# Softmax rows divided on ScalarE before the transpose, the residual added by TensorE, and the energies put ahead of the transposes

## The reference

```python
# L2
energy = jnp.einsum('bci,bcj->bij', q, k)
attention = jax.nn.softmax(energy, axis=-1)
out = jnp.einsum('bcj,bij->bci', v, attention)
out = gamma[0] * out + xf
# L3
scores = jnp.einsum('nia,nib->nab', theta, phi) / jnp.sqrt(jnp.float32(c))
attn = jax.nn.softmax(scores, axis=-1)
f = jnp.einsum('nab,nib->nia', attn, g)
```

## Time and profile before

| | |
|---|---|
| median of 3 runs | 5754.26 us |
| the profiled execution | 5758.38 us, of which 5756.6 us lie between its first and last instruction |
| VectorE busy | 5060.5 us (88%) |
| TensorE busy | 4756.3 us (83%) |
| GpSimd busy | 4706.1 us (82%) |
| ScalarE busy | 3713.5 us (65%) |
| TensorE's mean granted clock | 0.929 |

### The profile page before, as it was taken

One profiled execution on the slowest core, in us unless ns is written; L12 is line 12 of the kernel. 1 busy time (PEld: TensorE's weight loads), 2 busy tenths in 40 slices (PEclk: granted clock), 3 DMA queues, 4 the chain that ended last, 5 costly groups with the idle time before them and its releaser, 6 DMA issues.

```text
span 5756.6 us, 61917 instructions
## 1 busy us (share of the span) xinstructions
PE 4756.3 (83%) x17331; PEld 2758.9 (48%) x17331; DVE 5060.5 (88%) x5978; ACT 3713.5 (65%) x6077; POOL 4706.1 (82%) x3342
## 2 busy tenths in 40 slices
PE   6568888888888888888888888888888888888771
PEld 6134554555445445545554454455455544544451
DVE  4689999999999999999999999999999999999933
ACT  3456666667666666666676667666766766666633
POOL 0698988888888888888888988888888889888910
PEclk9679999999999999999999999999999999999995
DMA  4456555555565555656655655655566566555527
GB/s 130 182 219 223 221 201 218 220 220 211 217 220 211 209 221 216 218 208 220 220 204 219 223 215 211 218 216 204 219 220 220 208 219 225 212 207 219 214 82 295
DMA packets 199099, 1216.87 MB, mean 211 GB/s; under 512 B 27880, under 2 KB 28656, under 8 KB 67696
## 3 DMA queue, kind: packets, MB, share of 16 engines
q1 hardware_dynamic: 194416, 1196.26, 56.6%
q10 hardware_dynamic: 4352, 16.78, 0.7%
HBM read 1158.43 MB, written 54.53 MB: 211 GB/s over the span
## 4 chain that ended last, share of the span: by engine, by line
PE 34%; DVE 29%; issue 14%; ACT 12%; POOL 8%; DMA 1%; DVEq 1%; SPq 0%; POOLq 0%; ACTq 0%
DVE hs L488 12%; PE psE L814 12%; DVE psD L484 11%; PE psA L814 10%; PE psT L814 6%; POOL pa L300 5%; DVE nm L513 3%; PE psT L987 3%; ACT da L680 3%; ACT p L726 3%; PE psY L814 2%; DVE psU L477 1%; POOL pa L306 1%; ACT L649 1%; ACT L751 1%
## 5 line engine op out<-in xcount | busy, mean ns | idle before, releaser
L300 POOL TENSOR_TENSOR pa<-hs,rows_all 128x1024 f32<-128x1024 f32 x1024 | 2411.3, 2355 | 522.7 <-DVE hs L488 522.2
L680 ACT ACTIVATE da<-delta,neg_a 128x512 f32<-128x512 f32 x2048 | 1375.7, 715 | 224.9 <-DVE hs L488 212.6
L484 DVE TENSOR_TENSOR psD<-rows_all,psU 128x512 f32<-128x512 f32 x2048 | 1415.9, 691 | 84.6 <-POOL hlast L304 6.0
L488 DVE TENSOR_TENSOR_SCAN hs<-da,hlast,psD 128x512 f32<-128x512 f32 x1024 | 1310.8, 1280 | 36.3
L306 POOL TENSOR_TENSOR pa<-pa 128x512 f32<-128x512 f32 x1024 | 1301.2, 1271 | 40.1
L488 DVE TENSOR_TENSOR_SCAN hs<-da,psD 128x512 f32<-128x512 f32 x1024 | 1249.2, 1220 | 35.2
L726 ACT ACTIVATE p<-psE,nm 128x1024 f32<-128x1024 f32 x512 | 569.6, 1113 | 633.8 <-DVE nm L513 633.8
L814 PE MATMUL psA<-pt,va 128*128 128x256 f32 x4096 | 954.2, 381 | 1.0 <-DVE x L531 0.6
L814 PEld LDWEIGHTS psA<-pt,va 128*128 128x128 f32 x4096 | 772.5, 192 | 194.9 <-issue 105.9
L513 DVE TENSOR_REDUCE nm<-psE 128x1 f32<-128x1024 f32 x512 | 618.6, 1208 | 275.5 <-PE psE L814 272.3
L690 ACT ACTIVATE pt<-psT 128x512 f32<-128x512 f32 x1024 | 554.9, 591 | 342.5 <-PE psT L987 332.8
(11 more groups left out here) (186 smaller groups left out, 5087.6 us busy)
## 6 DMA issues: line engine op xcount, KB each, us to landing
rows_all<-bc_scratch SPq DMA_DIRECT2D x1024, 1024.0 KB, 4.7
xin<-x SPq DMA_DIRECT2D x40, 512.0 KB, 7.8
xres<-x SPq DMA_DIRECT2D x64, 256.0 KB, 6.3
x_scratch<-x SPq DMA_DIRECT2D x32, 512.0 KB, 4.2
f_scratch<-fa SPq DMA_DIRECT2D x32, 512.0 KB, 6.8
xres<-x SPq DMA_DIRECT2D x8, 512.0 KB, 3.7
x1g<-x SPq DMA_DIRECT2D x8, 512.0 KB, 3.6
fa<-x SPq DMA_DIRECT2D x8, 512.0 KB, 3.7
```

What stands on the lines that cost most here:

```text
L300: pool.tensor_tensor(pa[:, k % PROD, :, :], hs[:, sl, :, :], rows_all[:, slot, 2:4, :], ALU.mult).then_inc(S["prod"], 1)
L484: dve.tensor_tensor(psD[:, :], rows_all[:, slot, j, :], psU[:, :], ALU.mult).then_inc(S["dbu_ok"], 1)
L488: dve.tensor_tensor_scan(hs[:, sl, j, :], da[:, sl, j, :], psD[:, :], hlast[:, h, n_:n_ + 1] if ch else 0.0, ALU.mult, ALU.add).then_inc(S ...
L680: act.activation(da[:, k % 2, j, :], delta[:, h, cols(ch)], ACT.Exp, scale=neg_a[:, h, 2 * q + j:2 * q + j + 1]).then_inc(S["da_ok"], 1)
```

## The change

- ScalarE multiplies the exponentials `p` of each tile in place by the reciprocals of their row sums (`scale`, 128x1024, 16 times an image), before TensorE transposes them. The transpose waits for it (semaphore `scaled`).
- VectorE takes one reciprocal column for a tile (16 an image, where it took two columns for a group, 8 an image), and takes it inside a step, between the second product and the second scan. For that `scans` is split into `inputs` and `states`.
- TensorE no longer spreads the reciprocals. For m = 0 it adds the residual x1g into psA with one matmul of 256 columns for a group; gamma goes into the values.
- ScalarE copies the finished group from psA to `x2` or `fa` (`weighed`), where it copied `rb`. VectorE keeps only `bn_stats` for m = 1.
- `ORDER`: the energy of a step stands ahead of the transpose, of `steps` and of `centre`.

```diff
-        RECIP_AT = [10, 13, 15, 18]
+        RECIP_AT = [8, 9, 11, 12, 14, 15, 17, 18]
...
                 def normalise(a, o):
-                    for m, gq in groups_at(RECIP_AT, o):
-                        i = NG // 2 * m + gq
-                        pair = slice(GT * (i % 2), GT * (i % 2) + GT)
-                        wait(dve, "p_ok", a, GT * (i + 1))
-                        wait(dve, "av_mm", a, i - 1)
-                        dve.reciprocal(rinv[:, pair], rsum[:, pair]).then_inc(S["rinv_ok"], 1)
+                    for m, t in tiles_at(RECIP_AT, o):
+                        i = TILES * m + t
+                        sl = slice(i % (2 * GT), i % (2 * GT) + 1)
+                        wait(dve, "p_ok", a, i + 1)
+                        wait(dve, "scaled", a, i - 2 * GT + 1)
+                        dve.reciprocal(rinv[:, sl], rsum[:, sl]).then_inc(S["rinv_ok"], 1)
...
-                        wait(dve, "av_mm", a, i + 1)
-                        wait(dve, "rb_ok", a, i + 1)
-                        if m == 0:
...
-                            dve.scalar_tensor_tensor(out=psA[:, 0:GL], in0=psA[:, 0:GL], scalar=c_gam, in1=rb[:, :],
-                                                     op0=ALU.mult, op1=ALU.mult).then_inc(S["scaled"], 1)
-                            wait(dve, "scaled", a, gq + 1)
-                            dve.tensor_tensor(x2[:, part], psA[:, 0:GL], x1g[:, part], ALU.add).then_inc(S["out_ok"], 1)
-                        else:
...
-                            dve.tensor_tensor(fa[:, part], psA[:, 0:GL], rb[:, :], ALU.mult
-                                              ).then_inc(S["out_ok"], 1)
+                        if m == 1:
...
+                def scale(a, o):
+                    for m, t in tiles_at(RECIP_AT, o):
+                        i = TILES * m + t
+                        rs = i % (2 * GT)
+                        wait(act, "rinv_ok", a, i + 1)
+                        act.activation(p[:, i % 2, :], p[:, i % 2, :], ACT.Copy, scale=rinv[:, rs:rs + 1]
+                                       ).then_inc(S["scaled"], 1)
+
+                def weighed(a, o):
...
-                        act.activation(rb[:, :], psA[:, GL:2 * GL], ACT.Copy).then_inc(S["rb_ok"], 1)
...
+                        act.activation((x2, fa)[m][:, part], psA[:, 0:GL], ACT.Copy).then_inc(S["out_ok"], 1)
...
                             for a, o in now:
+                                scale(a, o)
                                 turned_out(a, o)
...
                 def turn(a, m, t, front):
                     i = TILES * m + t
-                    wait(pe, "p_ok", a, i + 1)
+                    wait(pe, "scaled", a, i + 1)
...
                     if half:
-                        wait(pe, "rinv_ok", a, i + 1)
-                        for u in range(GT):
-                            rs = (GT * i + u) % (2 * GT)
-                            last = mm(psA[:, GL + 128 * u:GL + 128 * u + 128], rinv[:, rs:rs + 1].to_broadcast([128, 128]),
-                                      ident[:, :])
+                        if m == 0:
+                            wait(pe, "x1g_ok", a, NCH)
+                            last = mm(psA[:, 0:GL], ident[:, :], x1g[:, gq * GL:(gq + 1) * GL], start=False)
...
-                    "centre energy add variance",
-                    "energy turn add weigh0",
-                    "weigh1 turn add residual",
+                    "centre add variance",
+                    "add energy weigh0 turn",
+                    "weigh1 residual turn add",
...
-                    "steps energy add weigh0",
-                    "turn weigh1 turn_more skip1 add",
-                    "energy add",
-                    "energy turn weigh0 add",
-                    "turn weigh1 add",
+                    "add energy steps weigh0",
+                    "weigh1 turn skip1 turn_more add energy_next",
+                    "add",
+                    "weigh0 energy turn add",
+                    "weigh1 turn add energy_next",
```

More of the change, by code:

```diff
@@ L232, in build, with tiles_at @@
         TURN_AT = [8, 10, 12, 12, 14, 15, 17, 18]
-        RECIP_AT = [10, 13, 15, 18]
+        RECIP_AT = [8, 9, 11, 12, 14, 15, 17, 18]
         WEIGH_AT = [(11, 12), (14, 15), (17, 18), (19, 19)]
         ATTEND_AT = [13, 16, 18, 20]
+        def tiles_at(table, o):
+            return [(m, t) for m in range(2) for t in range(TILES) if 16 * m + table[t] == o]
         def turned_at(o):
-            return [(m, t) for m in range(2) for t in range(TILES) if 16 * m + TURN_AT[t] == o]
+            return tiles_at(TURN_AT, o)
         def groups_at(table, o):
@@ L468, in normed, with inputs @@
                     dve.tensor_tensor(xn[:, KC - 1 + fc * CH:KC - 1 + fc * CH + CH], xcen[:, :], rstd[:, :], ALU.mult).then_inc(S["xn_ok"], 1)
-                def scans(b, k, j):
+                def inputs(b, k, j):
                     ch, r = divmod(k, NS)
@@ L549, in image @@
                             if scan:
-                                scans(b, k, 0)
+                                inputs(b, k, 0)
+                                states(b, k, 0)
                             if front_of and r == AT_N:
                                 normed(*front_of)
-                            for a, o in now:
-                                normalise(a, o)
                             if att and k == 2:
@@ L561, in image @@
                             if scan:
-                                scans(b, k, 1)
+                                inputs(b, k, 1)
+                            for a, o in now:
+                                normalise(a, o)
+                            if scan:
+                                states(b, k, 1)
                             for a, o in now:
@@ L754, in image @@
                             for a, o in now:
-                                spread(a, o)
+                                weighed(a, o)
                             if att and k == 5:
@@ L999, in values @@
                     for j in range(TB // 2 * half, TB // 2 * (half + 1)):
[L1000 removed]
+                        last = mm(psA[:, 0:GL], va[:, j, :], pt[:, i % 2, j, :], start=(j == 0),
+                                  stop=(j == TB - 1 and m == 1))
                     if half:
[L1002 to L1006 removed]
+                        if m == 0:
+                            wait(pe, "x1g_ok", a, NCH)
+                            last = mm(psA[:, 0:GL], ident[:, :], x1g[:, gq * GL:(gq + 1) * GL], start=False)
                         last.then_inc(S["av_mm"], 1)
@@ L1044, in _ @@
                     "energy add",
-                    "energy turn add skip0",
-                    "gates add",
-                    "energy rows turn add",
-                    "steps energy add weigh0",
-                    "turn weigh1 turn_more skip1 add",
-                    "energy add",
-                    "energy turn weigh0 add",
-                    "turn weigh1 add",
+                    "skip0 energy turn add",
+                    "gates add energy_next",
+                    "rows turn add",
+                    "add energy steps weigh0",
[3 more added lines that the diff above has]
+                    "weigh1 turn add energy_next",
                 ]
@@ L1102, in work @@
                                             energy(a, *TILE_STEP[o], scan)
+                                        if what == "energy_next" and o + 1 in TILE_STEP:
+                                            energy(a, *TILE_STEP[o + 1], scan)
                                         if what in ("turn", "turn_more"):
```

30 lines of the change are left out of this document (16 added, 14 removed).

## The result

The changed kernel takes 5865.78 us (median of 6 runs, 5857.75 to 5871.87) against 5754.37 us of the kernel before beside it: a ratio of 1.0198, with a 95% interval of 1.0184 to 1.0211. It is slower by 111 us, where I had forecast 56. The time lies inside the range.

The account below looks back on a forecast made before the run. Bound by VectorE's summed work and, in steps 7 to 17, a loop between engines. Per image 2.3 + 2.0 + 2 x 0.8 - 2.4 - 1.7 = +1.8 us; 31 images +56, so 5810 us; range 5650 to 5880.

Parts of the forecast that it names:

- the side: Whole kernel: the change makes it slower, chance 0.50, against 0.14 for the same and 0.36 for faster.
- the loop: Steps 7 to 17 of each attention: energy, maximum, exponential, next energy set the end; seven scalings enter it.
- stretch A: End of tile 0's maximum to start of tile 4's: 2.3 us longer for m = 0, 2.0 for m = 1.
- stretch B: End of tile 4's maximum to start of tile 7's, 20.2 us before: 0.8 us longer in each attention.
- the gain of VectorE's queue: Work and waits that VectorE loses, less the new reciprocals: 201 us less if its queue set the end everywhere.
- The wait that I named: VectorE at tile 3's reciprocal, for sums of ScalarE's exponential: 1.7 us; all reciprocal waits some 80 to 150 us.
- stretch C: End of tile 7's maximum to start of the next attention's tile 0: -2.4 us for m = 0, -1.7 for m = 1.
- the clock: Tile 3's energy on TensorE, after a longer idle time: kept at 3.25 us, where another energy took 1.88.
- Rival 1: Clock stays up, energies of tiles 3 and 6 at full rate: -3.0 us an image, 5661 us; chance 0.22.
- `steps`: Step 11, now behind tile 3's energy: four activations end at 25.0 us, tile 3's exponential follows at 26.1, before 22.4.

Follow-up runs that it names:

- experiment 4: Changed kernel with the matmuls of `steps` put ahead of tile 3's energy again in step 11: 5776.96 us, ratio 1.0046.
- experiment 11: Kernel of experiment 5 with ScalarE's four activations of step 11 moved behind the exponential of tile 3: 5715.71 us, ratio 0.9934.
- experiment 9: Kernel of experiment 5 with ScalarE's scaling cut to 2 of the 1024 columns of each tile: 5659.9 us, ratio 0.9838.
- experiment 5: Changed kernel with tile 7's energy put ahead of `add` in step 17: 5802.12 us, ratio 1.0085.
- experiment 8: Changed kernel with four added, unused matmuls of 256 columns ahead of tile 3's energy in step 11: 5784.56 us, ratio 1.0059.
- experiment 7: Kernel before, with only the line of step 11 changed, so `add` and tile 3's energy stand ahead of `steps`: 5651.35 us, ratio 0.9823.
- experiment 10: Kernel before with the changed table ORDER, except step 17, which stays as it was: 5765.61 us, ratio 1.0023.
- experiment 3: Changed kernel with ScalarE's scaling cut to 2 of the 1024 columns of each tile: 5803.15 us, ratio 1.0094.

## Why the prediction was right and wrong

**Right: the side, the loop, and the length of stretches A and B; this in part by luck.** I had said that the gain of VectorE's queue would be given back where a tile's energy, maximum, exponential and scaling hang in a ring. Stretch A grew by 1.9 us (forecast 2.15) and B by 0.8 (0.8). The wait that I named, at the reciprocal of tile 3, is the largest. All waits before reciprocals are 214.3 us, where I had said 80 to 150. Experiments 4 and 11 undo its cause from two sides, TensorE's and ScalarE's, and the wait goes in both; they win 89 and 86 us, of which a part comes by other ways (stretch B in 11, and perhaps the clock in 4). The pass takes 1.148 us by the trace of the changed kernel (1.14 forecast), and its length costs 142 us in the kernel of experiment 9.

Luck has a share in three places. In A of m = 0 I had the energy of tile 3 1.2 us too long (3.25 for 2.07 in the mean), and the stretch is only 0.5 us shorter than forecast, so some 0.7 us of the other sign are not found. In A of m = 1 I had read one attention, 30.96 us, where the mean is 32.2; the changed kernel has 34.2 for the 33.0 of the forecast, so both ends were 1.2 us short and the difference came out. In B the +0.8 stood for energies at the low clock, but those of tiles 6 and 7 take 2.2 and 1.8 us. The maxima of these tiles wait 0.9 and 0.8 us for them in the mean, and tile 7's wait goes when its energy stands ahead of `add` (experiment 5).

**Wrong: the size of stretch C.** The step reads "m = 0: [...] 25.7 us, with TensorE ready at 25.3; -2.4" and "m = 1: [...] ready at 26.7; -1.7". It measured 27.2 in both, -0.8. Nothing of VectorE's saving counts there beyond what TensorE lets through; the maximum of tile 0 waits 1.05 and 1.44 us for its energy. I had TensorE's queue too short by 1.9 us in m = 0 and by 0.5 in m = 1. The trace of the kernel before shows it, in the same stretch of m = 0:

```profile
3109.73 1.96 PE L814 MATMUL psT<-x,tp_t 128*128 128x512 f32 x4 [0.88 <-issue]
...
3118.26 1.96 PE L814 MATMUL psE<-ka,x 128*128 128x512 f32 x4
```

Tile 0's energy ends at 3120.2, 27.8 us after the maximum of tile 7, and VectorE takes it at 28.1. So TensorE was only 0.3 us ahead before the change, and the change takes 0.6 us out of its queue (27.8 to 27.2), where I had it fall to 25.3. I left out the 0.88 us in which it waits, between the convolution and `project`, until ScalarE has emptied psT; in the changed kernel that copy is this row of ScalarE, and TensorE goes on at 3001.12:

```profile
3000.34 0.69 ACT L638 ACTIVATE xc<-psT,cbias 128x512 f32<-128x512 f32 x1 [4.08 <-PE psT L825]
```

The other 1.0 us I put down to small pieces (the edge columns, the residual's matmul, two short waits), without a row for each. That term is (2.4 + 1.7 - 1.6) x 31 = 77 us. Some 16 of it come from the one image that I had read, whose two stretches C, 28.1 and 28.4 us, are 0.5 us longer together than the means. The other differences have the other sign: A was 0.25 us an attention too dear, 16 us, and some 16 us come back outside the images. 77 - 16 - 16 = 45, the miss between the profiled executions (102 us for 56).

**Half right: the clock.** I let the energy of tile 3 run at 3.25 us in every attention. Over 57 attentions it takes 2.4 us, less than before the change, so this was too dark. What I had left out is what comes after it: `steps` and the first group at half rate, which in m = 1 put the four activations and the exponential of tile 3 later still. In sum the low clock in step 11 costs 81 us (experiment 8). Rival 1, with the clock up, was to give 5661 us; with the clock up in step 11 the kernel takes 5785. Its part A comes out in sum (+1.3 and -0.2 us, where it had +0.7 and +0.4), C was too short there as well (77 us), and B is 0.8 us longer than before, where it had nothing (50 us).

**Half right: `steps`.** In the prediction this line of the order only costs. In the changed kernel it does. In the kernel before the line wins 99 us (experiment 7), so it is bad only together with something that the change brings. That this is the scaling in its shadow is likely and not shown: the two orders were not compared with a short scaling, and `add` moved too. My theory for that experiment fell.

**The order and the division.** Alone, the order costs 127 us and the division 364. The order's loss in the kernel before is mainly step 17, 112 us, where tile 7's energy stands behind GpSimd's sum; I had that wait in part B, with nothing won as its price. In the changed kernel the swap wins 64 us, but most of it in stretch A (experiment 5). The line of step 2 costs 20 us, and those of steps 12, 14 and 15 cost 20. Of the 114 us that are left besides step 17, about 74 stay open: they lie in the lines of steps 0 and 8 (the energy ahead of `centre`, `skip0` first) or in the lines together. By the stretches, most of the 114 us are in C: 29.1 us in experiment 10, 27.4 in experiment 7.

## What to carry to other kernels

When work is moved off the busiest engine, look where it lands in the ring of waits, not at how busy the engine there is: ScalarE only went from 65% to 72%, and yet a pass of 1.15 us between an exponential and its transpose, with the waits around it, cost more than 138 us less on VectorE gave. The place of an independent instruction in a queue can be worth as much as an operation, and its sign depends on the rest of the kernel: the same line of the table won 99 us over the old one in one version and cost 89 in the other, so a reordering is tried alone, on each version. The time that it wins may come from elsewhere than the wait that it clears (experiments 5 and 11), so the stretches are measured again after each edit. Where an engine gets less work, add up the queue of the next one completely, with the waits that it already has, and compare the sum with the trace of before.

## What the runs showed of the hardware that I had not expected

- After 4 us with 1.65 us of work, TensorE ran for most of the next 12 us at 1.2 GHz, while it was busy all the time; in the kernel before a like gap was followed by 4 us with a granted clock of 0.70. Four unused matmuls in the gap, 2.0 us, kept it at 2.4 GHz, and the program became 81 us faster. In the kernel of experiment 7 they won nothing (10 us slower).
- A scaling by a column on ScalarE, 128x1024 in place, takes 1.148 us; cut to 2 columns it still takes 0.296 us (experiments 3 and 9). The Trainium skill, "ScalarE: Activation LUTs", section "What ACT_TABLE_LOAD costs", gives a fixed part, a part for each column operand and 0.833 ns an element, from which I estimate 1.13 and 0.28 us: the runs agree within 20 ns.
